# An attention stage that computes its weighted values turned around, in strips and halves of the matmul array

## The chip, the cores and the metric

The kernel runs on one core of one Trainium2 chip. The metric is the device time of one execution in microseconds (us), lower is better. All data are fp32 in the stage that is changed.

## What is computed

Two layers on 32 sequences of 68 tokens (36 image patches and 32 text tokens), 256 features wide. The change touches only the attention of the first layer, with 16 heads of 16 features and a window of 64:

```python
q = (x @ Wq + bq).reshape(B, S, H, hd).transpose(0, 2, 1, 3)
k = (x @ Wk + bk).reshape(B, S, H, hd).transpose(0, 2, 1, 3)
v = (x @ Wv + bv).reshape(B, S, H, hd).transpose(0, 2, 1, 3)
scores = jnp.einsum('bhqd,bhkd->bhqk', q, k) * scale
scores = jnp.where(allowed, scores, NEG_INF)
attn = jax.nn.softmax(scores, axis=-1)
out = jnp.einsum('bhqk,bhkd->bhqd', attn, v)
...
return out @ Wo + bo
```

x is the layer-normed input. Around it stand the patch embedding before, and after it a mixture of 64 experts, a second mixing layer computed through a discrete Fourier transform, and a mixture of 8 experts.

## The kernel before

The kernel is one program with hand-placed semaphores: each engine has its own instruction list, and a `wait_ge` holds that engine, and all that is queued behind it, until another engine has counted a semaphore up. The stage in question is `window_attention`. It handles the 32 sequences in 8 blocks of ABLK = 4. The 256 features are 2 chunks of 128 (DC = 2), so 8 heads (HC) lie in a chunk. One unit is one sequence and one chunk, and a block has UNITS = 8 units. Each step of the loop starts one unit and carries on three older ones (a software pipeline): the blocks 1 to 6 run in a hardware loop, the first and the last are written out.

For one unit the work is:

- GpSimd (POOL) spreads the keys (L427): `kheads` holds the 68 keys eight times, each copy masked by `head_of` to the 16 rows of one head, 128 rows by 8 x 68 columns.
- TensorE (PE) computes scores (L506): the 68 queries as stationary operand over all 128 rows, `kheads` moving, two matmuls of 272 columns. An fp32 matmul that isn't a transpose is two passes, that is two weight loads (PEld) and two MATMUL instructions, so this is 4 of each.
- VectorE (DVE) adds the mask (L553), takes the peak (L557) and subtracts it (L560); ScalarE (ACT) takes the exponential (L598).
- PE transposes the 8 head matrices of 68 x 68 (L479, 8 instructions), ACT moves them to `probsT` (L603).
- PE weighs (L488): for each head `probsT` (68 x 68) is the stationary operand, and the head's 16 value columns with a column of ones behind them are moving, 17 columns. The result `pout` has queries on 68 partitions, and for each head 16 sums and one total. That is 8 matmuls, 16 instructions.
- DVE inverts the 8 totals (L539, 68 x 8) and multiplies (L541, 68 x 128) into `outs`.
- PE transposes `outs` back (L461, or L527 after the last block) into `pjob`, and ACT adds the bias of v and places it in `aT` (L593). This is the job "out".

Between these lie the projections, also called jobs: v of one sequence (L466, 4 instructions of 256 columns, moved by ACT at L580) in the steps 0 to 3, and q and k of 128 features (L446, 4 instructions of 272 columns, moved by ACT at L585) in the steps 0, 1, 4 and 5. So the steps 0 and 1 of a block have two projections, 2 to 5 have one, and 6 and 7 have none. All jobs share one PSUM buffer `pjob`: each waits for `jobs_moved`, that ACT has moved the job before it.

The order in which PE takes a step is: job v if any, scores of unit s, job q or k if any, transposes of unit s-2, job "out" of unit s-4, weighing of unit s-3. `weigh` waits for `turn_moved` of its unit and for `normalised` of the unit before it, since `pout` is single. The scores wait for `keys_spread` of their unit and for `masked` of unit s-2. In the first block POOL also adds a bias to the residual (L412, three tiles in each step from step 2 on), and once a block it copies the next input block to `xb` (L437).

## Time and profile before

| | |
|---|---|
| median of 3 runs | 1192.36 us (1190.61 to 1192.55) |
| the profiled execution | 1186.31 us, of which 1184.5 us from its first to its last instruction |
| mean granted TensorE clock | 0.946 of full speed |
| attention stage in the trace | about 50 us to 294 us of the span |
| busy, whole span | PE 1042.7, PEld 863.1, DVE 642.9, ACT 438.1, POOL 572.3 us |

The profile shows for each engine when it worked, and for idle time what ended it. "PE" rows are the MATMUL instructions, "PEld" rows the loads of stationary operands, which overlap them. Matmuls are pipelined: the duration of one is longer than the distance from its start to the start of the next, so the pace of a row of n equal matmuls is (time of the merged row minus the duration of one) divided by n-1. In the timeline a merged row gives start, total time and count.

### The profile page before, as it was taken

Reading aid. Unit: us, or ns where it says so; the run is one execution under the profiler, and the core shown is the slowest. Engines: PE = TensorE matmul, PEld = TensorE weight load, DVE = VectorE, ACT = ScalarE, POOL = GpSimd, SP = SyncE. Lnnn points to the kernel's source line nnn. Section 1 sums busy time; section 2 is a strip of 40 time slices with the busy share of each in tenths; the row PEclk is TensorE's granted clock in tenths of the full one; section 3 lists DMA queues with packets and bytes.
Section 4 is the critical chain, followed back from the end, with each engine's and each line's share of the span. In section 5 each row is a group of like instructions: output and inputs, shape, how many; then the busy total and the mean of one; then the engine's idle time right before and its main releaser. Section 6 shows DMA issues by size and latency. Waiting matters only on the chain. (4 is left out here: it accounts for less than half of the span.)

```text
span 1184.5 us, 24732 instructions
## 1 busy us (share of the span) xinstructions
PE 1042.7 (88%) x7478; PEld 863.1 (73%) x7496; DVE 642.9 (54%) x1548; ACT 438.1 (37%) x1149; POOL 572.3 (48%) x754
## 2 busy tenths in 40 slices
PE   8699999998884699999999998479998957988996
PEld 6467777777673499999999998236555536888995
DVE  2487777775679577644444442677999651110111
ACT  2255555553244344444444441122332223323331
POOL 0183333331050578877777754777776002333332
PEclk9799999997998899999999998788999977999998
DMA  6100000000100576677898862334455012456342
GB/s 229 39 1 1 0 0 0 0 1 1 56 21 1 179 211 209 200 229 232 231 250 255 238 189 88 103 94 111 113 146 213 19 45 54 142 198 208 99 127 72
DMA packets 81174, 136.33 MB, mean 115 GB/s; under 512 B 19372, under 2 KB 58031, under 8 KB 78672
## 3 DMA queue, kind: packets, MB, share of 16 engines
q0 software_dynamic: 19584, 52.60, 17.0%
q1 hardware_dynamic: 32144, 55.90, 14.4%
q10 hardware_dynamic: 29376, 27.01, 6.6%
q8 instruction: 30, 0.49, 0.2%
q14 instruction: 40, 0.33, 0.1%
HBM read 195.35 MB, written 36.05 MB: 195 GB/s over the span
## 5 line engine op out<-in xcount | busy, mean ns | idle before, releaser
L1226 POOL DMA_INDIRECT x_x<-m_x_rows,x_idx x200 | 195.4, 977 | 67.1 <-issue 51.8
L1245 PE MATMUL x_pup<-x_xt,x_w 128*128 128x128 f32 x1600 | 212.6, 276 | 0.2 <-DMA x_w<-in_experts 0.2
L1245 PEld LDWEIGHTS x_pup<-x_xt,x_w 128*128 128x128 f32 x1600 | 195.7, 193 | 0.8 <-DMA x_w<-in_experts 0.6
L1491 POOL DMA_INDIRECT rl_y<-m_y_rows,rl_idx x136 | 135.6, 997 | 44.2 <-issue 36.6
L1309 DVE TENSOR_TENSOR x_hid<-x_gate,x_pup 128x128 f32<-128x128 f32 x200 | 57.7, 288 | 161.7 <-ACT x_gate L1281 158.8
L427 POOL TENSOR_TENSOR wa_kheads<-wa_kT,cst 128x544 f32<-128x544 f32 x64 | 73.0, 1150 | 133.2 <-PE wa_scores L506 87.5
L1254 PE MATMUL x_pdown<-x_w,x_hid 128*128 128x256 f32 x400 | 119.4, 381 | 0.2 <-DVE x_y L1316 0.2
L1277 ACT ACTIVATE x_xt<-x_pturn 128x256 f32<-128x256 f32 x200 | 76.7, 383 | 91.1 <-PE x_pturn L1237 83.3
L2232 DVE TENSOR_TENSOR x_y<-x_pdown,late_b 128x256 f32<-128x256 f32 x24 | 10.2, 425 | 172.7 <-PE x_pdown L2176 172.7
L2164 PE MATMUL x_pup<-x_xt,late_w 128*128 128x128 f32 x768 | 92.3, 280 | 11.7 <-DMA late_b<-in_b 9.3
L2164 PEld LDWEIGHTS x_pup<-x_xt,late_w 128*128 128x128 f32 x768 | 90.6, 195 | 15.9 <-issue 15.2
L2217 ACT ACTIVATE x_hid<-x_pup,late_b 128x128 f32<-128x128 f32 x192 | 54.6, 368 | 117.3 <-PE x_pup L2164 117.2
L1281 ACT ACTIVATE x_gate<-x_pup 128x128 f32<-128x128 f32 x200 | 55.4, 277 | 98.9 <-PE x_pup L1245 97.6
L2176 PE MATMUL x_pdown<-late_w,x_hid 128*128 128x256 f32 x384 | 86.7, 379 | 0.0
L1237 PE MATMUL x_pturn<-cst,x_x 128*128 128x128 f32 x400 | 77.7, 276 | 8.5 <-DMA x_x<-m_x_rows,x_idx 8.3
L1316 DVE COPY x_y<-x_pdown 128x256 f32<-128x256 f32 x200 | 83.6, 419 | 0.6 <-PE x_pdown L1254 0.5
L1237 PEld LDWEIGHTS x_pturn<-cst,x_x 128*128 128x128 f32 x400 | 56.2, 142 | 29.8 <-DMA x_x<-m_x_rows,x_idx 10.4
L2176 PEld LDWEIGHTS x_pdown<-late_w,x_hid 128*128 128x128 f32 x384 | 71.2, 190 | 8.6
L2128 POOL DMA_INDIRECT out_h<-x_y,m_ids_out x24 | 24.2, 1009 | 107.0 <-DVE x_y L2235 107.0
L1804 DVE SCALAR_TENSOR_TENSOR h<-rl_y,m_wt,h 128x256 f32<-128x256 f32 x136 | 66.5, 489 | 14.0 <-DMA rl_y<-m_y_rows,rl_idx 9.8
L488 PE MATMUL wa_out<-wa_vals,wa_probsT 68*68 68x17 f32 x1024 | 73.9, 215 | 0.0
L506 PE MATMUL wa_scores<-wa_kheads,wa_qT 128*68 128x272 f32 x256 | 70.5, 398 | 0.9 <-POOL wa_kheads L427 0.7
(281 smaller groups left out, 1866.9 us busy)
## 6 DMA issues: line engine op xcount, KB each, us to landing
x_w<-in_experts SPq DMA_DIRECT2D x200, 384.0 KB
late_w<-in_w SPq DMA_DIRECT2D x52, 1024.0 KB, 12.1
m_y_rows<-x_y ACTq DMA_DIRECT2D x200, 128.0 KB
m_x_rows<-xn SPq DMA_DIRECT2D x34, 128.0 KB, 1.8
x_x<-m_x_rows,x_idx POOLq DMA_INDIRECT x200
late_b<-in_b SPq DMA_DIRECT2D x24, 128.0 KB
patches<-in_patches SPq DMA_DIRECT2D x3, 864.0 KB, 12.4
rl_y<-m_y_rows,rl_idx POOLq DMA_INDIRECT x136, 2.8
```

The lines of the kernel that those rows point to most:

```text
L427: nc.gpsimd.tensor_tensor(kheads[:, step % 2, :, :], kT[:, c, b * S:(b + 1) * S].unsqueeze(1).broadcast_to([P, HC, S]), head_of, ALU.mult) ...
L488: mm = nc.tensor.matmul(pout[0:S, hd * VW:(hd + 1) * VW], probsT[:, slot2, hd, :], vals[:, img, c * HC + hd, :], start=True, stop=True)
L506: mm = nc.tensor.matmul(bank, qT[:, c, b * S:(b + 1) * S], kheads[:, step % 2, 4 * g:4 * g + 4, :].rearrange("p m n -> p (m n)"), start=Tr ...
L1226: nc.gpsimd.indirect_dma_start(x[:, s, :], None, x_rows, bass.IndirectOffsetOnAxis(ap=idx[:, s:s + 1], axis=0))\
L1237: mm = nc.tensor.transpose(pturn[:, bank, c * P:(c + 1) * P], x[:, s, c * P:(c + 1) * P], ident)
L1245: mm = nc.tensor.matmul(pup[:, bank, m * P:(m + 1) * P], w[:, s, (m * DC + c) * I0:(m * DC + c + 1) * I0], xt[:, s, c * P:(c + 1) * P], st ...
L1254: nc.tensor.matmul(pdown[:, s % 2, 0:D], hid[:, s, :], w[:, s, UP:W], start=True, stop=True).then_inc(down_done, 1)
L1277: nc.scalar.activation(xt[:, s, :], pturn[:, bank, 0:D], ACT.Copy).then_inc(turn_moved, 1)
L1316: nc.vector.tensor_copy(y[:, s, :], pdown[:, s % 2, 0:D]).then_inc(down_moved, 1)
L1491: nc.gpsimd.indirect_dma_start(y[:, t % YR, kk, :], None, y_rows, bass.IndirectOffsetOnAxis(ap=idx[:, n:n + 1], axis=0))\
L2164: mm = nc.tensor.matmul(pup[:, s, half, f * P:(f + 1) * P], w1[:, s, c, (half * HB + f) * P:(half * HB + f + 1) * P], xt[:, s, c * P:(c + ...
L2176: mm = nc.tensor.matmul(pdown[:, s, 0:D], hid[:, s, f, :], w2[:, s, f, :], start=(f == 0), stop=(f == FC1 - 1))
```

## The change

- Weighing is turned around. For each head the values are now the stationary operand and `probsT` is moving (68 columns), so the result has features on partitions and queries on columns, and needs no transpose. The stationary operand is 32 columns wide: 16 value columns and 16 zero columns (or, for the other four heads, zeros first and values behind). Head j writes to output partitions 32(j mod 4) to 32(j mod 4)+31: four column strips of the array, each used by two heads that accumulate into one PSUM region. The totals come from a second set of matmuls of the same form, with a constant of 16 ones and 16 zeros in place of the values. So a unit has 16 matmuls, 32 MATMUL instructions and 32 loads, where it had 8, 16 and 16.
- DVE inverts 128 x 68 totals and multiplies 128 x 68. The multiply also waits for `placed` of unit u-2, since ACT now reads `outs`.
- The job "out" is gone; ACT adds the bias and places straight from `outs`, at the end of its step.
- Scores are computed in two row halves: four matmuls of 136 columns, each over 64 rows of the array, alternately the lower and the upper 64. `kheads` has 4 head copies instead of 8, so POOL spreads 128 x 272 elements.
- Each step has one projection, behind the scores: k1, q1, v0, v1, v2, v3, k0, q0 (the last two not in the last block). The wait of the keys of step 0 is on q0, the last of them. The copy to `xb` moves from step 5 to step 6.
- DVE sets `vals` (68 x 2304) to zero and makes the ones at the start. The order of the heads' features is permuted in `Wo` and the bias of v outside the kernel.

The core of the diff:

```diff
-        "head_of": (p // HD == np.arange(HC)[None, :]) * 1.0,
+        "head_of": (p % (P // 2) // HD == np.arange(HC // 2)[None, :]) * 1.0,
...
-    VW = HD + 1
+    TILE = 2 * HD
+    BANK = HC // 2 * TILE + HD
+
+    def head_cols(c, m):
+        bank = 2 * c + m // (HC // 2)
+        first = bank * BANK - bank % 2 * HD + m % (HC // 2) * TILE
+        return slice(first, first + TILE)
...
-        kheads = sb("kheads", [P, 2, HC, S])
-        vals = sb("vals", [S, ABLK, H, VW])
+        kheads = sb("kheads", [P, 2, HC // 2, S])
+        vals = sb("vals", [S, ABLK, 2 * DC * BANK])
+        ones = sb("ones", [S, 3 * HD])
         probs = sb("probs", [S, 4, HC, S])
         probsT = sb("probsT", [S, 2, HC, S])
         peak = sb("peak", [S, 2, HC])
-        invsum = sb("invsum", [S, 2, HC])
-        outs = sb("outs", [S, 2, P])
+        invsum = sb("invsum", [P, 2, S])
+        outs = sb("outs", [P, 2, S])
...
+        JOBS = [("k1", 1), ("q1", 1), ("v", 0), ("v", 1), ("v", 2), ("v", 3), ("k0", 0), ("q0", 0)]
+        first_jobs, mid_jobs = list(enumerate(JOBS)), list(enumerate(JOBS))
+        last_jobs = list(enumerate(JOBS[:-2])) + [None, None]
+        n_first, n_mid = len(JOBS), len(JOBS)
...
-                nc.gpsimd.memset(vals[:, :, :, HD:VW], 1.0).then_inc(ones_set, 1)
-                head_of = k["const"]("head_of").unsqueeze(2).broadcast_to([P, HC, S])
+                head_of = k["const"]("head_of").unsqueeze(2).broadcast_to([P, HC // 2, S])
                 pool.wait_ge(w_in, 112)
...
-                            pool.wait_ge(jobs_moved, job_count(blk, number(table, "k1") + 1))
+                            pool.wait_ge(jobs_moved, job_count(blk, JOBS.index(("k1", 1)) + 1))
...
-                            kT[:, c, b * S:(b + 1) * S].unsqueeze(1).broadcast_to([P, HC, S]),
+                            kT[:, c, b * S:(b + 1) * S].unsqueeze(1).broadcast_to([P, HC // 2, S]),
...
-                        if step == 5 and table is not last_jobs:
-
-                            pool.wait_ge(jobs_done, job_count(blk, last_value(table) + 1))
+                        if step == 6 and table is not last_jobs:
+                            pool.wait_ge(jobs_done, job_count(blk, JOBS.index(("v", 3)) + 1))
...
-                    if kind == "out":
-                        unit = blk * UNITS + which - 4
-                        pe.wait_ge(normalised, unit + 1)
-                        nc.tensor.transpose(pjob[:, 0:S], outs[:, which % 2, :], ident[0:S, 0:S]).then_inc(jobs_done, 1)
-                    elif kind == "v":
+                    if kind == "v":
...
-                    for hd in range(HC):
-                        mm = nc.tensor.matmul(pout[0:S, hd * VW:(hd + 1) * VW], probsT[:, slot2, hd, :],
-                                              vals[:, img, c * HC + hd, :], start=True, stop=True)
+                    if first:
+                        pe.wait_ge(vals_set, 2)
+                    for sums in range(2):
+                        for hd in range(HC):
+                            rows = slice(hd % (HC // 2) * TILE, (hd % (HC // 2) + 1) * TILE)
+                            late = hd // (HC // 2)
+                            of = ones[:, late * HD:late * HD + TILE] if sums else vals[:, img, head_cols(c, hd)]
+                            mm = nc.tensor.matmul(pout[rows, sums * S:(sums + 1) * S], of, probsT[:, slot2, hd, :],
+                                                  start=(late == 0), stop=(late == 1))
                     mm.then_inc(weighted, 1)
...
-                        before, behind, late = table[step]
-                        if before:
-                            do_job(blk, *before)
+                        if step == 0:
+                            pe.wait_ge(jobs_moved, job_count(blk, 0))
                         pe.wait_ge(keys_spread, blk * UNITS + step + 1)
                         if not (start and step < 2):
                             pe.wait_ge(masked, blk * UNITS + step - 1)
                         if step == 4:
-                            pe.wait_ge(jobs_moved, job_count(blk, number(table, "k1") + 1))
-                        for g in range(2):
-                            bank = pscore[0:S, step % 2, g, 0:4 * S]
-                            mm = nc.tensor.matmul(bank, qT[:, c, b * S:(b + 1) * S],
-                                                  kheads[:, step % 2, 4 * g:4 * g + 4, :].rearrange("p m n -> p (m n)"),
+                            pe.wait_ge(jobs_moved, job_count(blk, JOBS.index(("q1", 1)) + 1))
+                        for quarter in range(4):
+                            m, g = quarter // 2 * 2, quarter % 2
+                            half = slice(g * P // 2, (g + 1) * P // 2)
+                            mm = nc.tensor.matmul(pscore[0:S, step % 2, g, m * S:(m + 2) * S], qT[half, c, b * S:(b + 1) * S],
+                                                  kheads[half, step % 2, m:m + 2, :].rearrange("p m n -> p (m n)"),
                                                   start=True, stop=True)
                         mm.then_inc(scored, 1)
-                        if behind:
-                            do_job(blk, *behind)
+                        if table[step]:
+                            do_job(blk, *table[step])
                         unit = blk * UNITS + step
...
-                        if late:
-                            do_job(blk, *late)
...
-                done = job_count(NBLK - 1, n_last)
-                for step in range(4):
-                    pe.wait_ge(jobs_moved, done + step)
-                    pe.wait_ge(normalised, n_units + step - 3)
-                    nc.tensor.transpose(pjob[:, 0:S], outs[:, step % 2, :], ident[0:S, 0:S]).then_inc(jobs_done, 1)
+                for step in range(3):
                     if step < 2:
                         turn(n_units + step - 2, (step - 2) % 4, step % 2, False)
-                    if step < 3:
-                        v = (step - 3) % UNITS
-                        weigh(n_units + step - 3, (step - 3) % 2, v % ABLK, v // ABLK, False)
+                    v = (step - 3) % UNITS
+                    weigh(n_units + step - 3, (step - 3) % 2, v % ABLK, v // ABLK, False)
...
-                def normalise(unit, slot):
+                def normalise(unit, slot, early=False):
                     dve.wait_ge(weighted, unit + 1)
-                    out3 = pout[0:S, 0:HC * VW].rearrange("q (m v) -> q m v", v=VW)
-                    nc.vector.reciprocal(invsum[:, slot, :], out3[:, :, HD]).then_inc(inverted, 1)
+                    nc.vector.reciprocal(invsum[:, slot, :], pout[:, S:2 * S]).then_inc(inverted, 1)
                     dve.wait_ge(inverted, unit + 1)
-                    nc.vector.tensor_tensor(outs[:, slot, :].rearrange("q (m v) -> q m v", v=HD), out3[:, :, 0:HD],
-                                            invsum[:, slot, :].unsqueeze(2).broadcast_to([S, HC, HD]),
-                                            ALU.mult).then_inc(normalised, 1)
+                    if not early:
+                        dve.wait_ge(placed, unit - 1)
+                    nc.vector.tensor_tensor(outs[:, slot, :], pout[:, 0:S], invsum[:, slot, :], ALU.mult)\
+                        .then_inc(normalised, 1)
...
+                nc.vector.memset(vals[:, :, :], 0.0).then_inc(vals_set, 1)
+                nc.vector.memset(ones[:, :], 1.0).then_inc(ones_all, 1)
+                dve.wait_ge(ones_all, 1)
+                nc.vector.memset(ones[:, HD:2 * HD], 0.0).then_inc(vals_set, 1)
...
-                        nc.scalar.activation(vals[:, which, :, 0:HD],
-                                             pjob[0:S, 0:D].rearrange("s (m v) -> s m v", v=HD),
+                    if kind == "v":
+                        if isinstance(blk, int) and blk == 0 and which == 0:
+                            act.wait_ge(vals_set, 1)
+                        by_tile = vals[:, which, :].rearrange("s (b x) -> s b x", x=BANK)[:, :, 0:HC // 2 * TILE]\
+                            .rearrange("s b (j y) -> s b j y", y=TILE)
+                        nc.scalar.activation(by_tile[:, :, :, 0:HD],
+                                             pjob[0:S, 0:D].rearrange("s (b j v) -> s b j v", b=2 * DC, v=HD),
...
-                    nc.scalar.activation(aT[:, c, bass.ds(at_blk * CB + b * S, S)], pjob[:, 0:S], ACT.Identity,
-                                         bias=bv[:, c:c + 1]).then_inc(jobs_moved, 1)
+                    act.wait_ge(normalised, blk * UNITS + step - 3)
+                    nc.scalar.activation(aT[:, c, bass.ds(at_blk * CB + b * S, S)], outs[:, step % 2, :], ACT.Identity,
+                                         bias=bv[:, c:c + 1]).then_inc(placed, 1)
...
-                        before, behind, late = table[step]
-                        if before:
-                            move_job(blk, *before)
                         if not (start and step < 1):
                             exp(unit - 1, (step - 1) % 4)
-                        if behind:
-                            move_job(blk, *behind)
+                        if table[step]:
+                            move_job(blk, *table[step])
                         if not (start and step < 2):
                             move_turned(unit - 2, step % 2)
-                        if late:
-                            move_job(blk, *late)
+                        if not (start and step < 4):
+                            place_out(blk, step)
...
+    head_rows = np.arange(H * HD).reshape(DC, 2, HC // 2, HD).transpose(0, 2, 1, 3).reshape(-1)
...
-        "wq": rows(L0_attn_Wq), "wk": rows(L0_attn_Wk), "wv": rows(L0_attn_Wv), "wo": rows(L0_attn_Wo),
-        "bq": cols(L0_attn_bq), "bk": cols(L0_attn_bk), "bv": cols(L0_attn_bv), "bo": np.asarray(L0_attn_bo)[None, :],
+        "wq": rows(L0_attn_Wq), "wk": rows(L0_attn_Wk), "wv": rows(L0_attn_Wv), "wo": rows(np.asarray(L0_attn_Wo)[head_rows]),
+        "bq": cols(L0_attn_bq), "bk": cols(L0_attn_bk), "bv": cols(np.asarray(L0_attn_bv)[head_rows]), "bo": np.asarray(L0_attn_bo)[None, :],
```

## Rows read from the trace of the kernel before

**Rows 1.** Stretch totals, 86 to 258 us: length, PE, PEld, DVE, ACT, POOL, clock, DMA.
```profile
86.00:258.00 172.00, 168.26 (x1585) 132.85 (x1584) 129.05 (x240) 89.85 (x192) 58.33 (x55) 1.00 0.00 0
```

**Rows 2.** Waits in the same stretch: total us, times, longest.
```profile
POOL wa_kheads L427 <- PE wa_scores L506: 75.0, 30, 3.5
DVE wa_probs L553 <- PE wa_scores L506: 27.2, 36, 1.3
```

**Rows 3.** Groups by line, same stretch: count | busy us, mean ns | idle before.
```profile
L488 PE MATMUL wa_out<-wa_vals,wa_probsT 68*68 68x17 f32 x768 | 53.6, 212 | 0.0
L506 PE MATMUL wa_scores<-wa_kheads,wa_qT 128*68 128x272 f32 x192 | 53.0, 398 | 0.8 <-POOL wa_kheads L427 0.7
L479 PE MATMUL wa_turn<-cst,wa_probs 68*68 68x68 f32 x384 | 30.7, 223 | 0.0
L466 PE MATMUL wa_job<-late_w,wa_xb 128*68 128x256 f32 x96 | 25.6, 389 | 0.0
L446 PE MATMUL wa_job<-xT,late_w 128*128 x93 | 25.2, 393 | 0.0
...
L488 PEld LDWEIGHTS wa_out<-wa_vals,wa_probsT 68*68 68x68 f32 x768 | 51.1, 142 | 0.0
```

**Rows 4.** Timeline of PE, a step without a projection: start us, total us, count.
```profile
276.31 1.11 PE L506 MATMUL wa_scores<-wa_kheads,wa_qT 128*68 128x272 f32 x4
277.26 0.64 PE L479 MATMUL wa_turn<-cst,wa_probs 68*68 68x68 f32 x8
277.78 0.25 PE L461 MATMUL wa_job<-cst,wa_outs 68*128 68x68 f32 x1
277.91 1.13 PE L488 MATMUL wa_out<-wa_vals,wa_probsT 68*68 68x17 f32 x16
278.88 1.11 PE L506 MATMUL wa_scores<-wa_kheads,wa_qT 128*68 128x272 f32 x4
```

**Rows 5.** Timeline of PE, first scores of two neighbouring blocks.
```profile
141.45 0.90 PE L506 MATMUL wa_scores<-wa_kheads,wa_qT 128*68 128x272 f32 x3
...
170.17 1.13 PE L506 MATMUL wa_scores<-wa_kheads,wa_qT 128*68 128x272 f32 x4 [0.17 <-POOL wa_kheads L427]
```

**Rows 6.** Timeline of DVE in the step of Rows 4.
```profile
277.56 0.71 DVE L553 TENSOR_TENSOR wa_probs<-wa_scores,cst 68x544 f32<-68x544 f32 x1
...
279.69 0.20 DVE L539 RECIPROCAL wa_invsum<-wa_out 68x8 f32<-68x8 f32 x1
279.92 0.29 DVE L541 TENSOR_TENSOR wa_outs<-wa_out,wa_invsum 68x128 f32<-68x128 f32 x1
280.13 0.71 DVE L553 TENSOR_TENSOR wa_probs<-wa_scores,cst 68x544 f32<-68x544 f32 x1
```

**Rows 7.** Other reciprocals and small products of DVE: by line, min/median/max ns; a group.
```profile
L1326 DVE RECIPROCAL x_wsum<-x_wsum x1: 259/259/259, 406.9 to 406.9; 128x17 f32<-128x17 f32 x1
...
L727 DVE TENSOR_TENSOR m_rank<-m_pcount,m_base 128x64 f32<-128x64 f32 x1 | 0.2, 216 | 0.0
```

**Rows 8.** Timeline of PE later: matmuls of 16 columns or rows beside full ones.
```profile
812.76 1.09 PE L1515 MATMUL rl_pz<-xT,late_w_a 128*16 128x272 f32 x4
813.78 0.87 PE L1526 MATMUL rl_pv<-late_w_v,xT 128*68 128x256 f32 x3
...
934.92 0.81 PE L1583 MATMUL rl_pv<-m_chosen_b,m_before_b 128*128 128x512 bf16 x3
935.66 0.31 PE L1541 MATMUL rl_pz<-cst,rl_z 16*68 16x16 f32 x4
```

**Rows 9.** The stage's end: stretch totals (columns as Rows 1), timeline.
```profile
282.00:294.00 12.00, 8.40 (x68) 8.00 (x68) 2.22 (x9) 3.05 (x7) 0.00 (x0) 0.52 0.01 1
...
286.62 0.35 PE L527 MATMUL wa_job<-cst,wa_outs 68*128 68x68 f32 x1 [0.71 <-DVE wa_outs L541]
...
293.50 0.32 ACT L593 ACTIVATE m_aT<-wa_job,late_b 128x68 f32<-128x68 f32 x1 [2.48 <-PE wa_job L527]
```

**Rows 10.** Group by line on POOL, whole span: a product of 256 columns.
```profile
L412 POOL TENSOR_TENSOR h<-h,late_b 128x256 f32<-128x256 f32 x17 | 14.3, 864 | 0.0
```

36 lines of the change are left out of this document (5 added, 31 removed).

## The prediction

> **What bounds the kernel now.** I read the stretch totals first. From 86 to 258 us of the span, in the middle of the attention stage, PE is busy 168.3 of 172.0 us, DVE 129.1, ACT 89.9 and POOL 58.3 [rows 1]. The waits say the same from the other side: POOL waits for the scores 75.0 us in that stretch and DVE 27.2 us [rows 2], while the groups of PE show next to no idle time [rows 3]. So PE sets the pace there, and nobody else works on anything that would cover a longer stage: what PE's step gains or loses goes into the kernel's time one to one. The next view is the timeline of one step with no projection, which gives each part of a unit by the distance between starts [rows 4]: scores 277.26 - 276.31 = 0.95 us, transposes 0.52, job "out" 0.13, weighing 0.97, together 2.57. DVE in the same step also needs 280.13 - 277.56 = 2.57 us with no idle time between its rows [rows 6]: it is the second bound, and stands close behind. A whole block takes 170.17 - 141.45 = 28.72 us [rows 5]. A projection of 272 columns costs what the scores cost, 0.95 (also four passes of 272 columns), one of 256 columns 256/272 of it, 0.89. The block's terms are 8 x 2.57 + 4 x 0.95 + 4 x 0.89 = 27.9 us, so 0.8 us a block are seams, where PE waits for a moved job, a spread key or the loop.
>
> **Paces.** The sixteen weighing passes start (1.13 - 0.21)/15 = 61 ns apart, the eight transposes (0.64 - 0.22)/7 = 60 ns [rows 3, 4]. The transposes move 68 columns; the weighing moves only 17 but loads 68, and its loads run beside its matmuls: mean 142 ns for a load and 212 ns for a matmul, at 61 ns a pair. So a pass costs the larger of its loaded and its moving columns, some 0.87 ns each (0.95/4/272).
>
> **The change, part by part, for a unit.**
> - Scores: eight passes of 136 columns instead of four of 272. One after the other they cost the same, 8 x 0.118 = 0.95. If the two row halves work at once, only the two passes of one matmul follow each other in their half, the second beside the first of the next quarter: five passes in a line, 0.59. The trace has no two matmuls on different rows, so the ends are 0.59 and 0.95; I take 0.59, since the quarters alternate halves and banks and share nothing that the trace shows to be busy.
> - Weighing: 32 passes instead of 16, each now loads 32 columns and moves 68, 60 ns like a transpose. One after the other 32 x 0.060 = 1.92 us. If strips work at once, the two passes of one head still share a strip and follow each other, while the second runs beside the first of the next head: about 16 x 0.060 = 0.96. No row shows two strips at work, so 0.96 and 1.92 are the ends. I take 1.05, the lower end with a little for issue: the loads pace at half of today's, 32 x 28 ns = 0.9 us, and aren't the limit. Turned around, the weighing alone therefore gains nothing even at its best; it only makes the next term possible.
> - Job "out": its 0.13 us go, and with it its place in the queue for `pjob`. Its placing stays on ACT, which has 172 - 90 us to spare [rows 1] and does it last in its step, so nothing of PE waits behind it; the multiply's new wait on `placed` is for a unit two steps older. Of the 0.8 us of seams a block I count 0.4 off, since each step has one job and each finds the one before it moved; bounds 0 and 0.8.
> - Switching between full array, halves and strips. Ordinarily the next matmul starts 0.12 to 0.17 us before the end of the merged row ahead of it [rows 4]. Behind the matmuls of 16 columns it starts 812.76 + 1.09 - 813.78 = 0.07 us before, and ahead of those of 16 rows 934.92 + 0.81 - 935.66 = 0.07 [rows 8]. Both of these sit at a change of the part of the array in use, and both lose some 0.09 us. After the change a step has three such seams (into the scores, out of them, into the weighing). I take 0.11 each, 0.33 in all; bounds 0 and 0.6.
> - Transposes stay, 0.52. Sum 0.59 + 0.52 + 1.05 + 0.33 = 2.49 against 2.57: 0.08 x 64 units = 5.1 us less, and seams 8 x 0.4 = 3.2.
> - The projections are the same in number and size; they are only spread one to a step. That would pay where the light steps are held by another engine; they are held by PE as much as by DVE [rows 4, 6], so I count nothing. k1 and q1 come a step and more before they are used. The close one is q0 in step 7: POOL's spreading for the next block waits for it. From the job's start 0.95 + 0.2 to its end, ACT's move 0.47 (its mean, [rows 1]), POOL under 0.86 [rows 10], 2.5 us; PE has the job, transposes, weighing and two switches before it wants the keys, 0.95 + 0.52 + 1.05 + 0.22 = 2.7. Hidden, with 0.2 us to spare; if not, up to 0.5 us a block, 4 us. The copy to `xb` in step 6 has until step 2 of the next block.
> - POOL's spreading gets cheaper and has idle time anyway. In the first block it also carries the bias tiles, three of 0.86 us a step beside a spreading of 1.15 [rows 10]: 3.7 us, about PE's pace. It only gets shorter.
> - DVE: the reciprocal takes 0.20 us for 8 columns [rows 6] and 0.259 for 17 [rows 7], 6.6 ns a column, so 68 columns give 0.20 + 60 x 0.0066 = 0.59, +0.39. The multiply falls from 0.29 at 128 columns to the 0.216 of a product of 64 [rows 7]. DVE's step grows from 2.57 to 2.9. PE's mean step after the change is 2.49 + 0.92 + 0.05 = 3.5, so DVE stays hidden by 0.6 us; it is the floor beneath any better case. Setting `vals` to zero lies before the first scores, where DVE has nothing else.
> - [...] From 286.62 to 290.3 each step goes weighing, DVE, transpose of `outs`, next weighing. Without that transpose the chain loses its wait and 0.35 us, and gets DVE's 0.3 back. Bounds: nothing, or 6 us if the clock stays up; I take 3.
>
> Sum on the profiled execution: 1186.3 - 5.1 - 3.2 - 3 = 1175.0 us. The median of the runs is 6.05 us above the profiled execution, so 1181 us.
>
> [...] The trace shows a loss of 0.09 us at two changes of array part [rows 8]. [...] With no such loss the sum would be 64 x 0.33 = 21 us lower.
>
> **The rivals.**
> - Strips do not overlap, halves do: weighing 1.92, 0.87 x 64 = 56 us more, 1237 us. Neither overlaps: another 0.36 x 64 = 23, 1260. This is the other side, one mechanism: fp32 passes into different parts of the array are taken one at a time. It decides from 0.18 us a unit (11.3/64), that is a weighing pair above (1.05 + 0.18)/32 = 38 ns. [...] Against it: loads and matmuls do overlap.
> - Only the halves fail: 23 us more, 1204.
> - A load waits for the matmul in flight. Then a weighing pair costs load and pass, 28 + 60 = 88 ns, 2.8 us a unit, 112 us more than my sum: about 1293. Against it: today's loads and matmuls of the same rows interleave at 61 ns a pair [rows 3]. [...]
> - DVE takes over: the reciprocal is steeper than 17 columns tell. It decides from a DVE step of 3.5 us, a reciprocal of 1.2 us; then the time is about today's, 1190.
> - Everything packs better and DVE is the pace, 2.9 and a seam: 8 x 3.0 = 24 us a block against 28.72, 28 us in the six full blocks, 2 in the first and last, 5 at the end: 1157. This is the low end of my own case.
>
> **How the numbers follow.** My case, both overlaps, has 0.62, with its own range 1157 to 1200 (dear switches and no gain in seams at the upper end): 0.53 of it faster, 0.04 within, 0.05 slower. Halves alone fail 0.05; strips fail 0.10; neither overlaps 0.14; loads wait 0.04; DVE takes over 0.05 (0.02 faster, 0.02 within, 0.01 slower). That makes 0.55 faster, 0.06 within 0.2% (2.4 us, about what a measurement can tell from no change), 0.39 slower. The range 1158 to 1255 leaves out the very best packing, most of the case without any overlap and the waiting loads, some 0.17.
>
> **What would show it.** In the profile after: 32 weighing passes about 33 ns apart, not 60 (right) or 88; eight score passes in some 0.6 us of starts; a seam of about 0.1 us at each switch; the reciprocal near 0.59 us and DVE still waiting for PE each step; no L461 rows; a block near 27.7 us. The prediction is wrong if the weighing takes over 1.3 us a unit, if the clock falls in the stage, or if DVE's rows run without a gap.

## The result: 1162.1 us, a ratio of 0.9705

| | before | after |
|---|---|---|
| median of 4 runs each | 1192.45 us | 1162.09 us (1156.34 to 1164.80) |
| ratio | | 0.9705, 95% interval 0.967 to 0.9741 |
| profiled execution, its span | 1186.31, 1184.5 us | 1161.90, 1160.1 us |
| mean granted TensorE clock | 0.946 | 0.935 |
| first scores to first output projection | 236.5 us | 201.7 us |
| from there to the end | 890.4 us | 901.9 us |

The medians differ by 30.4 us where 11 were forecast. The ratio on record is not the quotient of these two medians, which would be 0.9745 and lies just outside its interval; taken from the ratio, the gain is 35 us (31 to 39), about what the stage gains, and in the later runs before took 1197 to 1200 us on chips of this speed. So the gain of the whole kernel lies somewhere from 30 to 39 us, and the stage is read more sharply than that. Of jobs_as_before and strips_full_rows, below, the first profiled execution was a slow one of its kernel (1287.1 us beside 1267.7, 1282.7 beside 1263.5), so there the second run decides.

Below, "the stage" is the time from PE's first scores to its first matmul of the output projection, and "the rest" is what follows.

Stretch total of after (us, PE, PEld, DVE, ACT, POOL, clock, DMA share, GB/s), then its waits and groups by line in the same stretch; they answer to [rows 1 to 3].

```profile
86.00:236.00 150.00, 140.13 (x2563) 105.52 (x2560) 142.67 (x249) 86.47 (x197) 46.12 (x56) 1.00 0.00 1
```
```profile
ACT wa_probs L587 <- DVE wa_probs L542: 63.2, 50, 1.7
POOL wa_kheads L415 <- PE wa_scores L495: 56.0, 32, 3.0
POOL wa_kheads L415 <- ACT wa_qT L573: 32.1, 6, 5.4
```
```profile
L542 DVE TENSOR_TENSOR wa_probs<-wa_probs,wa_peak 68x544 f32<-68x544 f32 x50 | 38.9, 779 | 1.7
...
L495 PE MATMUL wa_scores<-wa_kheads,wa_qT 64*68 64x136 f32 x396 | 34.0, 290 | 2.5 <-POOL wa_kheads L415 2.2 <-issue 0.3
...
L520 DVE RECIPROCAL wa_invsum<-wa_out 128x68 f32<-128x68 f32 x50 | 28.5, 571 | 0.0
...
L477 PE MATMUL wa_out<-wa_probsT,wa_vals 68*32 68x68 f32 x784 | 21.9, 227 | 7.4 <-DVE wa_outs L524 4.0
L477 PE MATMUL wa_out<-wa_probsT,wa_ones 68*32 68x68 f32 x784 | 21.8, 223 | 0.0
...
L524 DVE TENSOR_TENSOR wa_outs<-wa_out,wa_invsum 128x68 f32<-128x68 f32 x50 | 11.4, 229 | 2.2
```

The reader is to see that the two engines have changed places. DVE is busy 142.7 of 150.0 us, no row of it waits for PE any more (before: 27.2 us, [rows 2]), and the one large wait on DVE's work, 63.2 us, is ACT's. The 1568 weighing passes, of 49 units, take 43.7 us together, where the 768 of 48 units took 53.6 [rows 3].

Timeline of one step of after, PE and DVE (start us, total us, count):

```profile
141.55 0.57 DVE L520 RECIPROCAL wa_invsum<-wa_out 128x68 f32<-128x68 f32 x1
141.75 0.64 PE L462 MATMUL wa_turn<-cst,wa_probs 68*68 68x68 f32 x8
142.16 0.23 DVE L524 TENSOR_TENSOR wa_outs<-wa_out,wa_invsum 128x68 f32<-128x68 f32 x1
...
142.32 0.72 DVE L535 TENSOR_TENSOR wa_probs<-wa_scores,cst 68x544 f32<-68x544 f32 x1
...
142.53 0.44 PE L477 MATMUL wa_out<-wa_probsT,wa_vals 68*32 68x68 f32 x16
142.76 0.45 PE L477 MATMUL wa_out<-wa_probsT,wa_ones 68*32 68x68 f32 x16
...
143.08 0.72 DVE L539 TENSOR_REDUCE wa_peak<-wa_probs 68x8 f32<-68x544 f32 x1
143.14 0.68 PE L495 MATMUL wa_scores<-wa_kheads,wa_qT 64*68 64x136 f32 x8
143.76 1.08 PE L449 MATMUL wa_job<-late_w,wa_xb 128*68 128x256 f32 x4
143.83 0.72 DVE L542 TENSOR_TENSOR wa_probs<-wa_probs,wa_peak 68x544 f32<-68x544 f32 x1
144.47 0.57 DVE L520 RECIPROCAL wa_invsum<-wa_out 128x68 f32<-128x68 f32 x1
```

DVE's five rows follow each other without a gap, 144.47 - 141.55 = 2.92 us, against 2.57 in [rows 6]. PE starts weighing 0.78 us behind its transposes, where 0.57 would do (short_reciprocal, below), because it waits until DVE has freed `pout` (142.16 + 0.23). The eight steps of the block take 2.82, 3.60, 2.93, 2.92, 2.92, 2.92, 2.92 and 3.42 us, a block 24.44, where it was 28.72 [rows 5].

The block's edge in after. The last step of a block is 3.42 us because PE then waits 0.43 for the keys of the next; the long second step, 3.60, is explained further down.

```profile
126.55 0.47 ACT L573 ACTIVATE wa_qT<-wa_job,late_b 128x272 f32<-128x272 f32 x1
...
127.19 1.24 POOL L415 TENSOR_TENSOR wa_kheads<-wa_kT,cst 128x272 f32<-128x272 f32 x2 [5.36 <-ACT wa_qT L573]
...
127.96 0.68 PE L495 MATMUL wa_scores<-wa_kheads,wa_qT 64*68 64x136 f32 x8 [0.43 <-POOL wa_kheads L415]
```

And the end of the stage, which answers to [rows 9]:

```profile
245.03 0.44 PE L477 MATMUL wa_out<-wa_probsT,wa_vals 68*32 68x68 f32 x16 [1.00 <-DVE wa_outs L524]
...
247.91 0.68 PE L477 MATMUL wa_out<-wa_probsT,wa_vals 68*32 68x68 f32 x16 [0.99 <-DVE wa_outs L524]
...
257.52 0.35 ACT L582 ACTIVATE m_aT<-wa_outs,late_b 128x68 f32<-128x68 f32 x1 [1.83 <-DVE wa_outs L524]
```

The last placing moved from 293.50 to 257.52. Counted from the first scores, 29.4 us are gained up to the start of the last block (7 blocks) and 5.4 in the last block and the end, 34.8 in all. The first block gains 3.1 us, less than the 4.3 of a later one; there the granted clock of after is low until 62.9 us, 6.4 us into the stage, and that of before rises at 57.2, ahead of its first scores.

### The profile page after: what moved, and what is told of

Read it like the earlier page. It is cut to its first block and busy times, and to the rows that moved or that the text cites. A ratio compares the mean times of both kernels' runs of the same rounds, so it can differ in the third digit from the quotient of the medians.

```text
span 1160.1 us, 27101 instructions
## 1 busy us (share of the span) xinstructions
PE 1012.9 (87%) x8712; PEld 829.4 (71%) x8712; DVE 659.4 (57%) x1551; ACT 432.2 (37%) x1149; POOL 546.8 (47%) x753
## 5 line engine op out<-in xcount | busy, mean ns | idle before, releaser
L415 POOL TENSOR_TENSOR wa_kheads<-wa_kT,cst 128x272 f32<-128x272 f32 x64 | 53.2, 836 | 102.4 <-PE wa_scores L495 62.9
L1787 DVE SCALAR_TENSOR_TENSOR h<-rl_y,m_wt,h 128x256 f32<-128x256 f32 x136 | 69.5, 511 | 12.6 <-DMA rl_y<-m_y_rows,rl_idx 8.3
L587 ACT ACTIVATE wa_probs<-wa_probs 68x544 f32<-68x544 f32 x64 | 42.1, 657 | 75.1 <-DVE wa_probs L542 75.0
L1237 PEld LDWEIGHTS x_pdown<-x_w,x_hid 128*128 128x128 f32 x400 | 60.9, 192 | 0.7 <-DVE x_hid L1292 0.6
```

The source lines that it names most:

```text
L1237: nc.tensor.matmul(pdown[:, s % 2, 0:D], hid[:, s, :], w[:, s, UP:W], start=True, stop=True).then_inc(down_done, 1)
L1787: nc.vector.scalar_tensor_tensor(h[:, t, :], y[:, t % YR, kk, :], wt[:, t, kk:kk + 1], h[:, t, :], ALU.mult, ALU.add).then_inc(added, 1)
```

## The experiments

The questions were: what each of the three parts (strips, halves, one projection in each step) is worth, why the weighing is so much cheaper than forecast, whether DVE is the pace, and what the spreading of the projections does, which the sum had counted at nothing. Some of the chips on which these kernels ran are slower: there the kernel before takes 1285 to 1288 us instead of 1192 to 1200. All of that lies in the rest (985 to 1000 us instead of about 900); in the stage a block at full clock takes the same time on both (27.14 us for halves_only, 25.74 for strips_full_rows). So I compare stages and blocks in us, and totals only by their ratio to before on the same chip. Of a kernel that ran twice the first run was on a slower chip and the second on a faster one; the filled one ran twice on faster ones. In the table the intervals of such pairs are the second run's.

| kernel | halves | strips | one job a step | stage us | block us | total, ratio to before |
|---|---|---|---|---|---|---|
| before | | | | 236.5 | 28.72 | 1 |
| spread_only | | | x | 257.1 | 30.16 | 1.0144 (1.0059 to 1.023) |
| halves_only, and _2 | x | | | 240.9, 232.2 | 27.14 | 0.9969, 0.9957 (0.9904 to 1.0011) |
| strips_only | | x | | 212.9 | 25.63 | 0.9803 (0.9724 to 0.9882) |
| strips_full_rows, and _2 | | x | x | 222.9, 216.0 | 25.74 | 0.9879, 0.9888 (0.9846 to 0.9931) |
| jobs_as_before, and _2 | x | x | | 226.7, 226.0 | 27.36, low clock in each | 0.9895 (0.9802 to 0.9987) |
| the same, filled, and _2 | x | x | | 208.9, 207.8 | 24.92 | 0.9732, 0.9777 (0.9694 to 0.9859) |
| after | x | x | x | 201.7 | 24.44 | 0.9705 (0.967 to 0.9741) |

A block is that of a stretch in which the clock stays at 1.00, except where it is said. The three kernels further down that leave out part of the computation are read by their stages and blocks; one_strip and two_strips ran once each, on a slower chip (1324.5 and 1264.1 us).

### How many strips work at once

```diff
-rows = slice(hd % (HC // 2) * TILE, (hd % (HC // 2) + 1) * TILE)
+rows = slice(0, TILE)
...
-start=(late == 0), stop=(late == 1))
+start=True, stop=True)
```

That is one_strip; two_strips has `slice(hd % 2 * TILE, (hd % 2 + 1) * TILE)` in its place. Both leave out part of the computation: the heads overwrite each other's sums, and the other strips of `pout` hold a constant.

> The changed kernel, but all eight heads of a unit write to the first strip (output partitions 0 to 31), and each overwrites the one before it; so the weighted values are left out for the other strips, and the same number and size of passes is issued. Theory A (a strip takes one 68-column pass in 59 ns, and four strips work at once): the 32 passes take 32 x 0.059 = 1.89 us a unit instead of 0.47, PE's step grows from 2.62 to about 4.04 us, PE takes over from DVE's 2.92, and the time is 1162 + 64 x 1.12 = 1234 us. Theory B (the short distance between passes comes from the narrow 32-column stationary operand, not from the strips): the passes stay about 15 ns apart on average and the time stays at 1162 us.

> The changed kernel with the heads alternating between two strips, each overwriting the last (part of the weighted values is left out). Theory A (one strip, one pass in 59 ns): 16 passes in each strip, 0.94 us a unit, PE's step 3.09 us, just above DVE's 2.92: 1162 + 60 x 0.17 = 1172 us. Theory B (narrow operands, not strips): 1162 us.

PE's timeline, first of one_strip, then of two_strips:

```profile
145.91 1.13 PE L477 MATMUL wa_out<-wa_probsT,wa_vals 68*32 68x68 f32 x16
146.88 1.11 PE L477 MATMUL wa_out<-wa_probsT,wa_ones 68*32 68x68 f32 x16
147.92 0.68 PE L495 MATMUL wa_scores<-wa_kheads,wa_qT 64*68 64x136 f32 x8
```
```profile
145.56 0.67 PE L477 MATMUL wa_out<-wa_probsT,wa_vals 68*32 68x68 f32 x16
146.06 0.64 PE L477 MATMUL wa_out<-wa_probsT,wa_ones 68*32 68x68 f32 x16
146.63 0.68 PE L495 MATMUL wa_scores<-wa_kheads,wa_qT 64*68 64x136 f32 x8
```

From the first to the last start of the 32 passes it is 1858 ns with one strip, 918 with two and 458 with four: 60, 30 and 15 ns a pass. The weighing scales with the number of strips, with no fixed part to be seen, so the narrow operand is not what makes the passes cheap. PE's steps are 4.11 to 4.22 us with one strip and 3.17 to 3.28 with two, where 4.04 and 3.09 were expected. The stage is 272.2, 216.8 and 201.7 us; from two strips to four only 15 us are left of the 0.46 x 64 = 29 that PE saves, since DVE's pace comes up in between.

### Does the order of the heads matter

```diff
-for hd in range(HC):
+for hd in (0, 4, 1, 5, 2, 6, 3, 7):
```

> The changed kernel with the heads weighed in the order 0, 4, 1, 5, 2, 6, 3, 7, so that neighbours in the list use the same strip; nothing else differs. Theory A1 (each strip has a queue of its own, and order in the list does not matter): weighing stays at 0.47 us a unit, 1162 us. Theory A2 (passes start in the order of the list, and one whose strip is busy holds up all behind it): only the change of strip after every two heads overlaps, the 32 passes take 1.2 to 1.7 us, PE's step becomes 3.4 to 3.8 us, and the time is 1162 + 60 x (0.4 to 0.9) = 1186 to 1216 us.

Two heads that share a strip now follow each other, so that four passes in a row go to one strip. The passes take 495 ns instead of 458, the block 24.47 us, the stage 201.9 (ratio 0.9695, 0.9617 to 0.9773). In after's records each strip starts a pass every 58 to 59 ns, and the neighbours' passes some 7 ns apart. The records don't name the strip, but a row of starts at that distance (0, 58, 117, 175, 234 ns and on) can be followed here too. So the strips behave like four queues, and a pass for a busy strip hardly holds up those behind it: held up, the set would have taken 1.2 us or more by the estimate in the expectation. The forecast's picture, in which the two passes of one head follow each other and everything behind them waits, is refuted.

### Is DVE the pace

```diff
-nc.vector.reciprocal(invsum[:, slot, :], pout[:, S:2 * S]).then_inc(inverted, 1)
+nc.vector.reciprocal(invsum[:, slot, 0:8], pout[:, S:S + 8]).then_inc(inverted, 1)
```

This inverts 8 of the 68 columns; the others are multiplied by one, so the result is left unnormalised there.

> The changed kernel with the reciprocal taken of 8 columns instead of 68; the other 60 columns of the inverted totals stay at 1, so most values are not normalised. Theory C (DVE is now the pace, 2.92 us a step, and PE's step is 2.62): the reciprocal falls from 0.57 to about 0.20 us, DVE's step to 2.55, PE takes over, and the time falls by 60 x 0.30 = 18 us to 1144 us. Rival (PE is still the pace and its wait before the weighing is only slack): no change, 1162 us.

PE's rows of one step:

```profile
144.20 0.44 PE L477 MATMUL wa_out<-wa_probsT,wa_vals 68*32 68x68 f32 x16
...
144.81 0.68 PE L495 MATMUL wa_scores<-wa_kheads,wa_qT 64*68 64x136 f32 x8
...
145.42 1.18 PE L433 MATMUL wa_job<-xT,late_w 128*128 x4
...
146.44 0.64 PE L462 MATMUL wa_turn<-cst,wa_probs 68*68 68x68 f32 x8
...
147.01 0.45 PE L477 MATMUL wa_out<-wa_probsT,wa_vals 68*32 68x68 f32 x16
```

The reciprocal falls from 571 to 200 ns, the block from 24.44 to 22.88 us, the stage to 189.4 (ratio 0.9622, 0.9544 to 0.9701). DVE was the pace. DVE's own step would now be 2.55, but the steps stop at 2.71 (with v) and 2.81 (with k or q), not at the 2.62 expected, so the stage gains 12.3 us instead of 18: here PE's own step is laid bare, weighing 0.61, scores 0.61, projection 1.02, transposes 0.57.

### What the spread projections do

```diff
-JOBS = [("k1", 1), ("q1", 1), ("v", 0), ("v", 1), ("v", 2), ("v", 3), ("k0", 0), ("q0", 0)]
+JOBS = [("v", 0), ("q1", 1), ("v", 1), ("k1", 1), ("v", 2), ("v", 3), ("q0", 0), ("k0", 0)]
+first_jobs = [(numbered[0], numbered[1]), (numbered[2], numbered[3]), (numbered[4], None), (numbered[5], None),
+              (None, numbered[6]), (None, numbered[7]), (None, None), (None, None)]
```

> The changed kernel with the projections placed as in the kernel before: v ahead of the scores in steps 0 to 3, q1 and k1 in 0 and 1, q0 and k0 in 4 and 5, none in 6 and 7. Theory A (two engines close together: a step costs the larger of DVE's 2.92 and PE's 1.75 plus 0.96 for each projection): steps 0 and 1 take 3.7 us, the others 2.92, a block 24.9 and up to 25.3 us against 24.44, stage 206 us. Rival (spreading the projections brings nothing, as the sum ahead of the result had it): stage 201.7 us.

> The kernel after with the projections where they stood before, once more, beside its filled version on the same chip. If the fall of the clock belongs to the sparse steps, it is there on any chip: a block 27.3 us, the stage about 227 us. If it belonged to the chip of the earlier run, the clock stays at 1.00 here, a block takes about 24.9 us and the stage about 208, like the filled version, and the even projections were worth only some 0.5 us a block.

It is the kernel after with the old places of the projections (and the copy to `xb` back in step 5). I had expected a stage of 206 us from DVE's pace alone, without any change of the clock. The block goes from 24.44 to 27.4 us on both chips, the stage to 226.7 and 226.0. Stretch totals and PE's timeline in jobs_as_before_2:

```profile
156.10:162.90 6.80, 5.77 (x118) 4.57 (x116) 6.56 (x12) 3.52 (x9) 2.45 (x3) 1.00 0.00 0
162.90:169.73 6.83, 5.86 (x52) 3.65 (x50) 5.15 (x10) 2.34 (x5) 1.46 (x2) 0.50 0.00 0
169.73:190.20 20.47, 19.45 (x369) 14.36 (x368) 17.66 (x32) 12.32 (x27) 5.80 (x8) 1.00 0.00 0
```
```profile
161.19 0.45 PE L480 MATMUL wa_out<-wa_probsT,wa_vals 68*32 68x68 f32 x16 [1.03 <-DVE wa_outs L527]
...
164.11 0.68 PE L480 MATMUL wa_out<-wa_probsT,wa_vals 68*32 68x68 f32 x16 [0.97 <-DVE wa_outs L527]
164.54 0.71 PE L480 MATMUL wa_out<-wa_probsT,wa_ones 68*32 68x68 f32 x16
165.18 1.98 PE L452 MATMUL wa_job<-late_w,wa_xb 128*68 128x256 f32 x4
```

In the steps without a projection PE waits 1 us for DVE. Then the granted clock falls to 0.50 and is back at 1.00 at 169.73; what falls into that time is the heavy start of the next block. The projection of v takes 1.98 us instead of 1.08. This comes back in every block. The next kernel puts two matmuls of no use into the steps 6 and 7 and changes nothing else:

```diff
+if step >= 6 and table is not last_jobs:
+    pe.wait_ge(jobs_moved, job_count(blk, len(JOBS)))
+    for c2 in range(DC):
+        nc.tensor.matmul(pjob[:, 0:CB], wk[:, c2, 0:P], xT[:, c2, bass.ds(blk * CB, CB)],
+                         start=(c2 == 0), stop=(c2 == DC - 1))
```

> The kernel after, with the projections put back where they stood before (two each in steps 0 and 1, none in steps 6 and 7), and with two matmuls of 272 columns of no use in each of the steps 6 and 7, into the projections' tile, except in the last block. My theory (TensorE's sparse steps 6 and 7 are what lets the granted clock fall to half, and the fall is most of what the uneven projections cost): the clock stays 1.00 through the stage, steps 0 and 1 take about 3.7 us, the others 2.92 (VectorE's pace), a block 24.9 to 25.3 us and the stage about 206 us, against 226.7 without the filling. The rival (it is the double load of steps 0 and 1 on TensorE that costs, and the clock is an accompaniment): steps 0 and 1 stay near 4 to 5 us, a block stays near 27.4 and the stage near 227.

> The same with two matmuls of 272 columns of no use in steps 6 and 7, on the same chip. If filling the sparse steps holds the clock up: 1.00 and a block of 24.9 us, as in its earlier run, whatever the version without filling does. If the chip decides: the same clock as the version without filling.

```profile
132.80:157.70 24.90, 24.79 (x428) 18.11 (x426) 22.78 (x41) 14.82 (x33) 7.34 (x9) 1.00 0.00 0
```

More work for PE, and the stage is 18 us shorter: 207.8 against 226.0 on the same chip. The two steps at the block's edge go from 5.28 and 5.13 us to 4.04 and 3.83, which is all of the difference of the block (2.54). The steps 2 to 6 take the same time in both. So of the 3.0 us a block which the spreading is worth here, 2.5 come from the clock staying up; the 0.5 left is the evenness itself and whatever the two added matmuls cost.

> The kernel before, with one projection in each step and nothing else changed (weighing, sums and scores as before). If spreading helps only by keeping the clock at full speed, it gains nothing here, since the clock was at 1.00 in the kernel before throughout the stage: TensorE remains the pace, a block 28.3 to 28.7 us, the stage 233 to 237 us against 236.5. If it evens the steps for VectorE as well, a block falls by up to 1 us.

Without the strips and the halves the same spreading costs time: I had expected 28.3 to 28.7 us a block. PE has no light step to win there (the clock of before was at 1.00 already, [rows 1]). At full clock the block takes 30.16 us instead of 28.72; the step at the edge alone goes from 3.85 to 4.88, where PE waits some 1.0 us for POOL's keys behind q0. The clock also fell at four places of the stage, which I didn't expect and can't explain by waits as above (ahead of the fall at 152.8 PE was busy 5.71 of 6.80 us); with that the stage is 257.1.

### The parts alone

> The kernel before with the weighing in four column strips and the sums by ones, but scores over all rows and the projections where they stood. Theory: strips alone gain the 0.45 us a step of the weighing only where TensorE has work; the steps 4 to 7 fall to VectorE's pace (2.9 us) and leave TensorE sparse, so the granted clock falls in each block, and the stage is about 228 us, of which the strips' gain by the counts alone would make about 212. Rival (the scores' halves are what lowers the clock, not the sparse steps): clock 1.00 and stage 212 to 216 us.

Strips alone are worth 3.1 us a block and 23.6 us of the stage. I had expected the clock to fall here too, and it didn't: the time came out as the rival had it (212 to 216 us). Stretch totals of PE's lightest 6.8 us in a block here, and then of 6.8 us in halves_only (below) at whose end the clock fell:

```profile
152.70:159.50 6.80, 5.69 (x130) 4.20 (x129) 6.56 (x12) 4.17 (x9) 2.55 (x3) 1.00 0.00 0
```
```profile
186.10:192.90 6.80, 6.65 (x84) 5.68 (x83) 5.70 (x12) 3.56 (x8) 0.64 (x1) 1.00 0.00 0
```

PE is as idle here as in jobs_as_before_2 ahead of its fall (5.77 of 6.80 us), and the clock stays up; in halves_only it is busy 6.65 of 6.80, and the clock falls. So PE's waits don't tell by themselves when the clock falls. That added matmuls in the light steps prevent it is shown by both filled runs; what it is in PE's work that decides is not. The row halves may have a part in it, as the rival said: before and strips_only, at full rows, keep 1.00 up to the last block, halves_only and jobs_as_before don't. But with one projection a step it is the other way round (below), so they aren't the cause alone.

The parts don't add up either. Strips with the old places of the projections make a stage of 212.9 us, with the halves beside them 226. With one projection a step, strips at full rows make 216.0, and with halves 201.7.

> The kernel before with the scores alone taken in two row halves (kheads of 4 copies, four matmuls of 136 columns); weighing, job out and the placing of the projections as before. The attention stage, first scores to the first matmul of the output projection, is 236.5 us before and 201.7 us in the changed kernel. Theory A (halves overlap; PE is the pace of the old kernel): the scores' part falls from 0.95 to 0.47 us of starts plus one pass, and two switches of 0.09 are added, so 0.2 us of 64 steps: stage about 224 us, total 12 us under before. Rival (the change works through the strips alone): stage 236 us, no difference.

> The kernel before with the scores in two row halves alone, once more. Its earlier run gained 0.5 us a block only, with the clock falling at four places of the stage. At full clock, by the measured spread of the scores (0.41 us instead of 0.72), it would gain 0.3 us a step less two switches of 0.09 us, some 1 us a block, and the stage would be about 228 us; if the clock falls here too, about 240.

Halves alone gain 1.6 us in a block at full clock, where the second text has about 1, but the clock fell at four places of the stage in one run and at three in the other, and the stages are 240.9 and 232.2 us; the first text had 224, with no fall of the clock. The total can't be told from no change (0.9957, 0.9904 to 1.0011).

> The changed kernel with the scores back over all 128 rows (two matmuls of 272 columns, kheads of 8 copies). Theory A (DVE is the pace at 2.92 us, PE works 2.7 to 2.8 us of it): PE's step rises by 0.33 and loses a switch of 0.09, to about 2.95, level with DVE; stage 204 us against 201.7, up to 206 because the keys' spreading at the block's start is longer by 0.4 us. Rival (each part of the change gives its own gain to the time): 12 us or more above, stage 214.

> The kernel after with scores over all rows, once more. If the falls of the clock of its earlier run (3.4 us in each block) were the chip's, its six steps at 3.0 us and the two at the edge at about 3.4 make a block of 25 us and a stage of about 206; if they belong to this kernel's work, a block is 27.4 again. Either way what the halves are worth beside the strips is the difference from the kernel after (24.44 us a block): 0.5 us at full clock, 3 us otherwise.

Timeline of the block's edge in strips_full_rows_2:

```profile
162.76 2.66 POOL L415 TENSOR_TENSOR wa_kheads<-wa_kT,cst 128x544 f32<-128x544 f32 x2 [4.47 <-ACT wa_qT L572]
164.50 1.13 PE L494 MATMUL wa_scores<-wa_kheads,wa_qT 128*68 128x272 f32 x4 [1.35 <-POOL wa_kheads L415]
```

I had expected a stage of 204 to 206 us. The clock fell in six of the first seven blocks on the slower chip, each time for 3.4 us, and in two on the other, though the steps ahead of it are the same: whether it falls differs for this kernel from block to block and from run to run. At full clock the block is 25.74, also more than the 25 expected. So beside strips and spreading the halves are worth 1.3 us a block: 1.07 at the edge (4.49 against 3.42), because POOL spreads half the columns and PE waits 0.43 us for them instead of 1.35, and the remainder because PE's step is 3.0 us, just above DVE's 2.92.

### The block's edge, and a better kernel

```diff
-pool.wait_ge(jobs_moved, job_count(blk, 0))
+pool.wait_ge(jobs_moved, job_count(blk, 0) - 1)
```

> The kernel after, with GpSimd's wait at the start of a block put on the projection of the keys (step 6) instead of that of the queries (step 7), which it does not read. If that wait is the edge's loss, the last step of a block falls from 3.42 to 2.9 us, the block from 24.44 to 23.9 us and the stage from 201.7 to about 199 us, at the least time that VectorE's pace allows. If VectorE is slowed there by GpSimd at work, or the queries are late themselves, the block stays at 24.3 to 24.4 us and the stage within 1 us of 201.7.

POOL no longer waits for the queries. The last step goes from 3.42 to 3.15 us, the block to 24.18, the stage to 200.1; the total is 0.9691 (0.9634 to 0.9748), not to be told from after. So that wait was worth 0.27 us a block, half of what I expected. (The stages' difference is no sharper measure of it: the clock, low when the stage begins, rises at 62.9 us of the span in after and at 60.6 here, and the first blocks take 23.25 and 22.29 us.) The other 0.8 us by which the block exceeds eight steps of 2.92 are DVE's own, as its rows in after show:

```profile
154.54 0.72 DVE L535 TENSOR_TENSOR wa_probs<-wa_scores,cst 68x544 f32<-68x544 f32 x1 [0.34 <-issue]
...
156.00 0.64 POOL L415 TENSOR_TENSOR wa_kheads<-wa_kT,cst 128x272 f32<-128x272 f32 x1 [2.04 <-PE wa_scores L495]
156.05 1.17 DVE L542 TENSOR_TENSOR wa_probs<-wa_probs,wa_peak 68x544 f32<-68x544 f32 x1
```

DVE loses 0.34 us where the hardware loop turns and 0.45 because its subtraction, which takes 0.72 alone, starts 0.05 us behind a product of POOL. With the order reversed POOL is the one that pays:

```profile
140.91 0.72 DVE L542 TENSOR_TENSOR wa_probs<-wa_probs,wa_peak 68x544 f32<-68x544 f32 x1
141.00 1.13 POOL L415 TENSOR_TENSOR wa_kheads<-wa_kT,cst 128x272 f32<-128x272 f32 x1 [1.79 <-PE wa_scores L495]
```

In both pairs the one that starts second takes longer, by 0.45 us (1.17 against 0.72) and by 0.49 (1.13 against 0.64), and the first keeps its time.

The subtraction of the peak can be done by POOL instead (the bias tiles of the first block are then spread over all of them):

```diff
+def shift(unit, slot4, slot2):
+    pool.wait_ge(peaked, unit + 1)
+    nc.gpsimd.tensor_tensor(probs[:, slot4, :, :], probs[:, slot4, :, :],
+                            peak[:, slot2, :].unsqueeze(2).broadcast_to([S, HC, S]),
+                            ALU.subtract).then_inc(shifted, 1)
```

> The changed kernel with the subtraction of the peak moved from DVE to POOL, and POOL's bias tiles spread over all blocks instead of the first. Theory C (DVE is the pace): DVE's step falls by 0.73 to about 2.2 us, PE takes over at 2.7 to 2.8 us, stage 189 us as with the short reciprocal, 12 us under the changed kernel. Rival 1 (POOL's subtraction costs over 1.9 us with the spreading of 0.84 beside it, or slows DVE's own work): no gain, or a loss, stage 202 us or more. Rival 2 (DVE was not the pace): stage 201.7 us.

> The kernel with the transposition (32x32 blocks) moved from VectorE to GpSimd, and with GpSimd's wait at the start of a block put on the projection of the keys (step 6) instead of that of the queries (step 7), which it does not read. Theory: the last long step of each block (3.27 us against 2.81 for the others) is the chain of query projection, ScalarE's copy and GpSimd's spreading of the keys; the block's edge falls to about 2.8 us, the block from 22.56 to 22.1 us and the stage from 187.3 to about 184 us. Rival: the queries are late themselves, or VectorE is slowed by GpSimd there, and the edge stays at 3.2 to 3.3 us and the stage at 187.

(The second text calls the moved operation a transposition; it is this subtraction.) The ratios are 0.9551 (0.9492 to 0.961) and 0.9557 (0.9499 to 0.9614), the second with a median of 1145.85 us, 16 us under after. The blocks are 22.56 and 22.34 us, the stages 187.3 and 184.7. Stretch total and one group of pool_shift_key_wait, then POOL's of pool_shift:

```profile
86.00:230.00 144.00, 143.15 (x2707) 108.88 (x2706) 113.39 (x208) 100.32 (x208) 102.55 (x127) 1.00 0.00 1
```
```profile
L404 POOL TENSOR_TENSOR wa_probs<-wa_probs,wa_peak 68x544 f32<-68x544 f32 x51 | 55.7, 1092 | 32.1 <-DVE wa_peak L551 32.1
L421 POOL TENSOR_TENSOR wa_kheads<-wa_kT,cst 128x272 f32<-128x272 f32 x52 | 33.2, 639 | 10.4 <-ACT wa_qT L581 10.4
```

PE is the pace again, busy 143.2 of 144.0 us, in steps of 2.71 and 2.81 as short_reciprocal laid them bare. The subtraction costs POOL 1.09 us where DVE took 0.72, but POOL has the time, and its products are all at 0.64 us now (mean 0.86 in after, the longest 1.14), since the subtraction beside which they took longer has left DVE. The relaxed wait brings the edge from 3.27 to 3.05 us, not to the 2.8 I expected.

### Did the rest of the kernel give something back

The rest is 11.5 us longer in the profile of after, though nothing in it is changed.

> The kernel before, unchanged, profiled a second time on another chip. If the change is what lengthens the rest of the kernel (from the first output projection of the attention stage to the end), the rest is 890 us again; if the first profile was a short one, it is 895 to 905 us, as in the ten profiles of changed kernels on chips of this speed, and the change gave nothing back there. The attention stage is 236.5 us either way.

It is the kernel before, unchanged. Stretch totals of the rest, of before_again and of after:

```profile
294.40:1196.00 901.60, 785.04 (x5220) 658.64 (x5220) 452.31 (x1156) 303.16 (x861) 478.61 (x657) 0.93 0.48 142
```
```profile
258.20:1160.00 901.80, 786.45 (x5220) 659.62 (x5220) 451.66 (x1156) 303.41 (x861) 472.49 (x657) 0.93 0.48 142
```

Its stage is 236.6 us, its rest 901.8: the first profile of before was a short one, with a granted clock of 0.94 in the rest against 0.93 in the two others, and the change gives nothing back that these profiles show. The profiles of before_again and of after differ by 36.1 us (1198.02 and 1161.90), the first two by 24.4 only; the medians' 30.4 lie between.

## Why the prediction was right and wrong

The direction and the order of events were right, the size was not: 30 us instead of 11.

- **Scores** in halves overlap as forecast. With their switch they take 0.61 us; the forecast was 0.59 + 0.11 = 0.70.
- **Weighing** is the term that failed, by its size: strips do work at once, as forecast, but a pass costs less than half of what was taken. With its switch it takes 0.61 us instead of 1.05 + 0.11 = 1.16. The step that failed is "the two passes of one head still share a strip and follow each other, while the second runs beside the first of the next head". The pairs of passes of different strips don't form one line; each strip has its own (15 ns a pass, not 33), and four strips divide the time by four. The lower end given for the unknown cost, 0.96, wasn't an end. The 0.55 us are 35 us over 64 units on PE.
- **Switches** were forecast at 0.11 each, and the rows bear that out roughly. In short_reciprocal the last pass of weighing starts 0.46 us behind the first, the scores 0.15 behind it, where the pace within a strip is 0.06: 0.09 us, as in [rows 8].
- **PE's step** is therefore 2.71 to 2.81 us, not 3.5, and the order of the engines turned over: "DVE stays hidden by 0.6 us" is wrong, "it is the floor beneath any better case" is right. DVE's terms were exact: the reciprocal 0.571 (0.59 forecast), the product 0.229 (0.216), the step 2.92 (2.9). PE's 35 us aren't the gain: the floor ended it at 19 us beyond the forecast by the medians, 24 by the stage. The text named DVE's rows running without a gap as a sign against itself, and they do.
- **The projections** were counted at nothing, "they are held by PE as much as by DVE". This was read from the steps of before. Once PE's light step is 1.8 us against DVE's 2.9, an uneven order leaves PE waiting, the clock falls, and the heavy steps pay: 3 us a block, 24 of the stage's 34.8, hang on that part of the change where strips and halves are both in. For the kernel before it was right that nothing is gained (spreading alone even costs 1.4 us a block at full clock); it was wrong to carry it over to a kernel with another bound. That the clock has a part in it was no term of the sum at all.
- **The close chain** of q0, ACT and POOL, "hidden, with 0.2 us to spare", isn't: PE waits 0.43 us a block, because it reaches the next scores earlier than 2.7 us behind the job. The upper bound of 0.5 us held.
- **Seams** weren't saved: 24.44 - 8 x 2.92 = 1.1 us a block, against 0.8 before, now on DVE.
- **The end of the stage** gave 5.4 us with the last block (4 forecast, 3 of it for the end). No run shows those 3 us by themselves, they were an estimate; what the runs show in their place is those 5.4 us, and a clock that is as low as before: 0.50 from 247.2 us of the span on in after, from 282.6 in before, in both until after the stage's end.
- **The rivals.** No pass waited for another part of the array, which removes the dear ones. A load doesn't wait for the matmul in flight either: 32 loads of the same rows run beside passes 15 ns apart, and on a single strip a load and its pass take 60 ns a pair (one_strip), not 88. The last rival, DVE as the pace with 24 us a block and 1157 us, is what happened: 24.44 and 1162. The text had it as the low end of its own case.

## What to carry to other kernels

Price a tiled form per strip, not per instruction: with two and four strips at work the row of short passes took a half and a quarter of the time (918 and 458 ns against 1858), and the bound of the case is then the next engine, whose step must be summed as carefully as the one that is being changed. When TensorE stops being the bound, look at the granted clock in every block of the new kernel: here light steps behind another engine's pace ended in a clock of 0.50 for the heavy steps that followed (jobs_as_before_2), and spreading the work evenly (after), or filling the light steps (the filled runs), kept it at 1.00. Don't add up the gains of parts that were measured one by one. Take the moved waits by the new step's length, not by the old one.

## What the hardware showed

- Four column strips run fully at once in fp32: 32 passes of 68 columns in 458 ns, 918 on two strips, 1858 on one; neighbouring strips start 7 ns apart, and the order in the list hardly matters (495 ns).
- Row halves likewise: eight passes of 136 columns start within 0.41 us, where four of 272 took 0.72.
- A switch of the array's division costs some 0.09 us (short_reciprocal).
- The clock fell to 0.50 behind 6.80 us in which PE was busy 5.77, with a gap of 1 us (jobs_as_before_2), and stayed at 1.00 when matmuls filled the light steps. It stayed at 1.00 around 5.69 busy of 6.80 in strips_only and fell behind 6.65 of 6.80 in halves_only, so PE's busy time alone doesn't decide. In strips_full_rows it fell in six blocks of one run and in two of the other.
- A reciprocal in fp32 costs 6.2 ns a column beyond the eighth ((571 - 200)/60, after and short_reciprocal).
- DVE's subtraction of the peak and POOL's spreading of the keys hold each other up (after): 0.72 us becomes 1.17, or POOL's 0.64 becomes 1.13. With the subtraction on POOL every spreading takes 0.64 (pool_shift).
- One kernel's unchanged 900 us of work can differ by 11 us between two profiles (890.4 and 901.8), beside another granted clock (0.86 and 0.78 from 900 to 1000 us). Small differences of two single profiles are no finding.
